# State-space heads: group sums of squares on VectorE, output products one slot later, decay sums split between GpSimd and ScalarE

## The reference, cut to what matters

```python
gate, hbc, dt = jnp.split(x @ in_proj_w.T, [I, I + CD], axis=-1)      # I = 32 * 128
hs, B, C = jnp.split(silu(causal_conv4(hbc) + conv_b), [I, I + G * N], axis=-1)
dt = softplus(dt + dt_bias);  A_cum = cumsum(-exp(A_log) * dt)        # along the sequence
# head h uses group h % 8 of B and C; over l >= s:
y[l] = sum_s (C[l] . B[s]) * exp(A_cum[l] - A_cum[s]) * dt[s] * X[s] + D * X[l]
h32 = y * silu(gate)
var = mean(h32 ** 2 over the 512 channels of a norm group (4 heads))
out = (norm_w * h32 * rsqrt(var + EPS)) @ out_proj_w.T
```

## Time and profile before

| what | us |
|---|---|
| median of 3 runs | 3315.8 (3304.01 to 3317.79) |
| the profiled execution's own time | 3299.21 |
| its span in the trace | 3297.4 |
| first half's heads, first `px` to last `px` | 148.8 to 640.8 |
| second half's heads, first `px` to last `px` | 766.6 to 1258.6 |
| TensorE busy over the span | 2619.4 (79%) |
| VectorE, ScalarE, GpSimd busy | 1809.8, 1525.4, 1227.2 |

### The profile page before, as it was taken

How to read it: one execution, slowest core, us unless ns; L and a number is a source line. 1 busy time by engine, 2 the same in 40 slices (tenths; PEclk the granted TensorE clock), 3 DMA queues, 4 the chain that set the end, 5 groups by cost and what they waited for, 6 DMA issues and landing times. The chain is left out here.

```text
span 3297.4 us, 47157 instructions
## 1 busy us (share of the span) xinstructions
PE 2619.4 (79%) x13661; PEld 1670.5 (51%) x13663; DVE 1809.8 (55%) x3839; ACT 1525.4 (46%) x2975; POOL 1227.2 (37%) x1164
## 2 busy tenths in 40 slices
PE   4799999987999996577777937878557749698884
PEld 2467777744777775344444523333244414365552
DVE  4666666674666664788882146776223342133234
ACT  3555555564555552588891114655235410233321
POOL 0477777635777773000000020000000027344443
PEclk8999999998999997666657957999679868799997
DMA  1121211002221210740000000000000024587885
GB/s 61 52 52 33 59 48 36 14 14 58 58 52 33 58 26 26 250 136 1 1 1 31 0 18 1 1 1 1 23 0 0 0 81 158 129 177 172 175 172 126
DMA packets 127073, 192.74 MB, mean 58 GB/s; under 512 B 17552, under 2 KB 88208, under 8 KB 125584
## 3 DMA queue, kind: packets, MB, share of 16 engines
q1 hardware_dynamic: 83696, 134.71, 14.5%
q0 software_dynamic: 23616, 33.24, 5.8%
q10 hardware_dynamic: 19584, 22.57, 2.5%
HBM read 123.23 MB, written 67.25 MB: 58 GB/s over the span
## 5 line engine op out<-in xcount | busy, mean ns | idle before, releaser
L234 DVE SCALAR_TENSOR_TENSOR h_pre<-h_px,h_par,h_pre 128x510 f32<-128x510 f32 (+2 forms) x384 | 286.5, 746 | 269.1 <-ACT h_pre L695 249.2
L658 PE MATMUL h_po<-h_wo,h_h 128*128 128x256 f32 x1024 | 328.2, 411 | 0.0
L580 POOL TENSOR_SCALAR h_decay<-h_cumb,h_sel 128x256 f32<-128x256 f32 x256 | 290.9, 1136 | 25.2 <-DMA h_cumb<-cum_rows 25.2
L591 POOL TENSOR_TENSOR h_mix<-h_decay,cb 128x768 f32<-128x768 f32 x128 | 232.8, 1819 | 165.0 <-ACT h_decay L681 165.0
L2890 POOL DMA_INDIRECT moe_sums<-ex_y,ex_sidx x132 | 204.8, 1552 | 234.7 <-DVE ex_y L3069 216.6
L622 PE MATMUL h_px<-x_cols,h_w 128*128 128x512 f32 x512 | 254.4, 620 | 25.3 <-DMA h_d<-d_skip 25.3
L849 POOL TENSOR_TENSOR norm_rstd<-norm_mv,mhalf 128x4 f32<-128x4 f32 x24 | 28.3, 1178 | 605.3 <-DVE norm_mv L832 605.3
L627 PE MATMUL h_pz<-x_cols,h_w 128*128 128x512 f32 x512 | 242.5, 596 | 5.6 <-DVE h_gate L748 5.6
L707 ACT ACTIVATE h_xt<-h_pxt,h_sel 128x128 f32<-128x128 f32 x512 | 145.9, 368 | 151.9 <-PE h_pxt L646 151.9
L2942 PE MATMUL ex_pg<-ex_w,ex_xT 128*128 x528 | 194.7, 492 | 25.6 <-ACT ex_xT L2998 10.5
L660 PEld LDWEIGHTS h_pss<-ones,h_sq 128*128 128x128 f32 x1024 | 194.6, 190 | 26.3
(11 more groups left out here) (389 smaller groups left out, 5809.6 us busy)
## 6 DMA issues: line engine op xcount, KB each, us to landing
h_cumb<-cum_rows SPq DMA_DIRECT2D x32, 1024.0 KB, 8.6
moe_tiles<-blank SPq DMA_DIRECT2D x4, 6642.0 KB, 44.2
ex_w<-moe_w SPq DMA_DIRECT2D x64, 352.0 KB
ex_xg<-moe_tiles ACTq DMA_DIRECT2D x136, 162.0 KB, 2.6
ex_wd<-moe_wd SPq DMA_DIRECT2D x64, 176.0 KB
h_w<-w_xg SPq DMA_DIRECT2D x8, 1024.0 KB, 10.5
moe_sums<-blank SPq DMA_DIRECT2D x2, 2176.0 KB, 26.6
h_wo<-w_out SPq DMA_DIRECT2D x8, 512.0 KB, 10.3
```

What stands on the lines that cost most here:

```text
L234: ins = dve.scalar_tensor_tensor(out=out[:, :, back:S], in0=src[:, :, 0:S - back], scalar=par[:, at + CK - 1 - back:at + CK - back], in1=o ...
L580: pool.tensor_scalar(decay[j][:, u, 0:S], cumb[s.vb][:, j, u, :], sel[s.vb][:, u * TPB, 1, j:j + 1], 0.0, ALU.subtract, ALU.min)
L591: pool.tensor_tensor(mix[j % 2][:], decay[j][:], cbj, ALU.mult).then_inc(matched, 1)
L658: pe.matmul(po[t // TPB][:, t % TPB, :], hh[j % 2][:, t * P:(t + 1) * P], w_out[s.pg][:, j, :], start=(j == 0 and t % TPB == 0), stop=(j = ...
```

## The change

- The loops and `LEAD` go: each engine's list is written out for all 16 steps, with constant counts and addresses. (The loops before ran once or twice around bodies that were written out as well.)
- `out` of head k moves from slot k to slot k+1, at the slot's end as before: `parts` of TensorE reads (-1, out). `hh` gets four buffers in place of two.
- The squares of j = 0 are written to a tile `sqs`, those of j = 1 to 3 to `sq`, and VectorE adds these three to `sqs` (`total`, one 128x512 instruction each, in the slot after the head's). TensorE multiplies `sqs` by the ones once per step, after the output product of j = 3.
- `variance` and `add` move from slot j = 0 to slot j = 1 of the next step on VectorE, `variance` ahead of the convolution, `add` behind the gate; `root` moves on GpSimd from slot j = 0, ahead of match and argue, to slot j = 1, behind them.
- GpSimd's `argue` writes only the two diagonal 128x128 blocks of each sequence (four instructions of 128x128); ScalarE's `decays` writes the block below the diagonal as Exp of `cumb` with the bias `less` (minus the column's sum, which `select` prepares), two instructions of 128x128, and then Exp of the diagonal blocks, one of 512 columns.
- `group` runs ahead of the first `argue`, and later in the middle of the group before; SyncE's `cumb` load waits for `decayed` in place of `argued`.

```diff
@@ Step, head_turns -> STEPS, head_slots (counts and addresses become constants) @@
+        less = [sb(f"less{i}", [P, TW, HG]) for i in range(2)]
-        hh = [sb(f"h{i}", [P, 2 * S]) for i in range(2)]
+        hh = [sb(f"h{i}", [P, 2 * S]) for i in range(HG)]
         sq = [sb(f"sq{i}", [P, 2 * S]) for i in range(2)]
+        sqs = [sb(f"sqs{i}", [P, 2 * S]) for i in range(2)]
...
@@ gpsimd @@
                 for u in range(2):
-                    pool.tensor_scalar(decay[j][:, u, 0:S], cumb[s.vb][:, j, u, :], sel[s.vb][:, u * TPB, 1, j:j + 1], 0.0,
-                                       ALU.subtract, ALU.min)
-                    ins = pool.tensor_scalar(decay[j][:, u, S:TRI], cumb[s.vb][:, j, u, P:S], sel[s.vb][:, u * TPB + 1, 1, j:j + 1], 0.0,
-                                             ALU.subtract, ALU.min)
+                    for b in range(TPB):
+                        ins = pool.tensor_scalar(decay[j][:, u, 2 * b * P:(2 * b + 1) * P], cumb[s.vb][:, j, u, b * P:(b + 1) * P],
+                                                 sel[s.vb][:, u * TPB + b, 1, j:j + 1], 0.0, ALU.subtract, ALU.min)
...
-                    if j == 0:
-                        root(prev)
-                    slot(parts, cur, nxt, j)
+            def body(k):
+                if k % (HG * NP) == HG * NP // 2 and k // HG + NP // 2 < len(STEPS):
+                    group(STEPS[k // HG + NP // 2])
+                slot(((2, match), (3, argue)), k)
+                if k % HG == 1 and k > HG:
+                    root(STEPS[k // HG - 1])
+
+            group(STEPS[0])
+            head_slots(-3, 0, body)
...
@@ tensor, out @@
-                pe.wait_ge(squared, LEAD + h + 1)
                 if j == 0:
-                    pe.wait_ge(added, LEAD + s.n)
+                    after(pe, added, s.n)
                 for t in range(TW):
-                    pe.matmul(po[t // TPB][:, t % TPB, :], hh[j % 2][:, t * P:(t + 1) * P], w_out[s.pg][:, j, :],
-                              start=(j == 0 and t % TPB == 0), stop=(j == HG - 1), skip_group_check=True)
-                    mm = pe.matmul(pss[:, t:t + 1], sq[j % 2][:, t * P:(t + 1) * P], r.ones[:, 0:1],
-                                   start=(j == 0 and t == 0), stop=(j == HG - 1), skip_group_check=True)
+                    mm = pe.matmul(po[t // TPB][:, t % TPB, :], hh[j][:, t * P:(t + 1) * P], w_out[s.pg][:, j, :],
+                                   start=(j == 0 and t % TPB == 0), stop=(j == HG - 1), skip_group_check=True)
                 mm.then_inc(outed, 1)
-            parts = ((3, project), (1, scan), (2, turn), (0, out))
+                if j == HG - 1:
+                    pe.wait_ge(totalled, (s.n + 1) * (HG - 1))
+                    after(pe, vared, s.n)
+                    for t in range(TW):
+                        mm = pe.matmul(pss[:, t:t + 1], sqs[s.vb][:, t * P:(t + 1) * P], r.ones[:, 0:1], start=True, stop=True)
+                    mm.then_inc(pooled, 1)
+            parts = ((3, project), (1, scan), (2, turn), (-1, out))
@@ scalar @@
-                act.activation(decay[j][:], decay[j][:], ACT.Exp).then_inc(decayed, 1)
+                for u in range(2):
+                    act.activation(decay[j][:, u, P:S], cumb[s.vb][:, j, u, P:S], ACT.Exp, bias=less[s.vb][:, u * TPB, j:j + 1])
+                own = decay[j][:].rearrange("p u (b l) -> p u b l", l=P)[:, :, 0:3:2, :]
+                act.activation(own, own, ACT.Exp).then_inc(decayed, 1)
...
@@ vector @@
+            def total(s, j, h):
+                if j:
+                    dve.wait_ge(squared, h + 1)
+                    dve.tensor_tensor(sqs[s.vb][:], sqs[s.vb][:], sq[j % 2][:], ALU.add).then_inc(totalled, 1)
...
-                    finish(*head(cur, nxt, j))
-                    if j == 0:
-                        variance(prev)
-                    slot(((2, silu),), cur, nxt, j)
-                    if j == 0:
-                        if nxt:
-                            select(nxt)
-                        add(prev)
-                    slot(((3, conv), (3, open_)), cur, nxt, j)
+                slot(((0, finish), (-1, total), (2, silu)), k)
+                if j == 0 and n + 1 < len(STEPS):
+                    select(STEPS[n + 1])
+                if j == 1 and n >= 1:
+                    variance(STEPS[n - 1])
+                slot(((3, conv), (3, open_)), k)
+                if j == 1 and n >= 1:
+                    add(STEPS[n - 1])
```

More of the change, by code:

```diff
@@ L414, with __init__, head_slots, at_head @@
 class Step:
[L417 to L442, removed]
+    def __init__(self, n):
+        self.n = n
+        self.g, self.p = divmod(n, NP)
+        self.g2, self.pg = divmod(self.g, 2)
+        self.two, self.vb = divmod(self.p, 2)
+STEPS = [Step(n) for n in range(GH * NP)]
+def head_slots(first, last, body):
+    for k in range(first, len(STEPS) * HG + last):
+        body(k)
+def at_head(h):
+    return (STEPS[h // HG], h % HG, h) if 0 <= h < len(STEPS) * HG else None
 def mamba_heads(nc, a, r, half, cum_rows, dtc, cb):
@@ L522, in mamba_heads, with slot, group @@
         block = ctx2.enter_context(nc.Block())
[L524 to L529, removed]
+        def slot(parts, k):
             for ahead, part in parts:
-                at = head(cur, nxt, j + ahead)
-                if at:
-                    part(*at)
+                if at_head(k + ahead):
+                    part(*at_head(k + ahead))
         @block.sync
         def _(sp):
-            def group(g2, pg):
-                sp.wait_ge(added, LEAD + (g2 * 2 + pg - 1) * NP)
-                g = (g2 * 2 + pg) * 2 + half
+            def group(s):
+                pg = s.pg
+                after(sp, added, (s.g - 1) * NP)
+                g = s.g * 2 + half
                 sp.dma_start(w_in[pg][:], a["w_xg"][g]).then_inc(loaded[pg], 16)
@@ L547, in cum, with group @@
             def cum(s):
-                sp.wait_ge(argued, LEAD + (s.n - 1) * HG)
+                after(sp, decayed, (s.n - 1) * HG)
                 sp.dma_start(cumb[s.vb][:].rearrange("p j u l -> p j (u l)"),
                              cum_rows[bass.ds((s.g * 2 + half) * HG, HG), bass.ds(s.p * 2 * S, 2 * S)].partition_broadcast(P)).then_inc(cums[s.vb], 16)
[L553 to L559, removed]
+            for s in STEPS:
+                if s.p == 0:
+                    group(s)
+                cum(s)
+            sp.wait_ge(added, len(STEPS))
         @block.gpsimd
         def _(pool):
-            for one in (scaled, matched, argued):
-                pool.drain().then_inc(one, LEAD)
             pool.memset(halves[:], 0.5)
             pool.drain()
-            pool.drain().then_inc(rooted, LEAD - 1)
-            def group(g2, pg):
-                pool.wait_ge(loaded[pg], (g2 + 1) * 64)
+            def group(s):
+                pg = s.pg
+                pool.wait_ge(loaded[pg], (s.g2 + 1) * 64)
                 pool.tensor_tensor(dskip[pg][:], dskip[pg][:], halves[:], ALU.mult)
@@ L593, in root @@
             def root(s):
[L594 to L595 removed]
+                pool.wait_ge(vared, s.n + 1)
+                after(pool, added, s.n)
                 pool.tensor_tensor(rstd[:], var[:], r.mhalf[:, 0:TW], ALU.pow).then_inc(rooted, 1)
[L598 to L604 removed]
@@ L606, in _ @@
-            for j in range(-3, 0):
-                slot(parts, Step(0, 0, 0, 0), None, j)
-            head_turns(pool, body, group)
-            root(Step(GH // 2 - 1, 1, NP // 2 - 1, 1))
+            def body(k):
[5 more added lines that the diff above has]
+            group(STEPS[0])
@@ L611, in _ @@
+            head_slots(-3, 0, body)
+            root(STEPS[-1])
         @block.tensor
         def _(pe):
-            for one in (projected, gprojected, turned, scanned, outed):
-                pe.drain().then_inc(one, LEAD)
             def project(s, j, h):
-                if s.opens and j == 0:
+                if s.p == 0 and j == 0:
                     pe.wait_ge(loaded[s.pg], (s.g2 + 1) * 64)
-                pe.wait_ge(convolved, LEAD + h - 1)
+                after(pe, convolved, h - 1)
```

130 lines of the change are left out of this document (58 added, 72 removed).

## The result

Slower, by less than forecast. The kernel after took 3332.1 us (median of 7 runs, 3317.0 to 3341.3), the kernel before 3314.0 beside it (7 runs, 3304.0 to 3317.8). The ratio is 1.0056 [1.0038, 1.0075]: +18 us where +45 were forecast. The profiled executions are 3328.4 and 3299.2, with spans of 3326.6 and 3297.4, +29.2. The heads carry nearly all of that: from the first `px` of a half to its last add, 514.0 and 514.1 us have become 528.7 and 525.9, together +26.6.

What follows compares the result with a forecast made beforehand. The heads were taken as bound by TensorE's own work. Waits +11.1, two steps without -5.4, starts -10.4 and clock +49.5 sum to +44.8 us, on the median 3315.8 giving 3361; range 3302 to 3395 (8 in 10).

Steps and rivals of the forecast that it cites:

- the chain: From the turn in slot j = 0 through ScalarE, GpSimd and VectorE to TensorE's output product: 10.87 us, 7.80 covered, 3.07 waited.
- TensorE's own work: In the heads, a step of four heads falls by 2.70 to 28.50 us, before any wait.
- which nothing gives back: Behind each of 30 new TensorE waits, a 3.3 us stretch at half clock loses 1.65 us: +49.5 us.
- The starts: At each half's start, TensorE's 3.56 us wait and the slow stretch behind it go: 5.2 each, -10.4 us.
- These I set to nothing, 0 to 5 us either way: Small effects, among them VectorE's `total`, ScalarE's extra time, GpSimd's `group` in mid-group and SyncE's loads: set to nothing.
- Rival one: In the heads, the same 3.07 us wait but the clock holds: 3311 us, no change; chance 0.15.
- Rival two: VectorE's queue alone sets the wait, about 2.3 us, clock kept: step 30.8, whole 3288 us; chance 0.13.
- Rival three: Two slow stretches behind each wait in the heads, +49.5 us more: 3410 us; chance 0.17.

Runs made afterwards that it cites:

- e5_onein: e1_early with GpSimd's match reading one tile: it copies the decay and leaves out the product with `cb`; 3203.6 us, 0.9654 of the kernel before.
- e3_fill: The kernel after with six products of 256 columns, results unread, put on TensorE ahead of the wait for the add; 3306.6 us, 0.9996 of the kernel before.
- e1_early: e2_root with the add moved right behind the variance, ahead of the convolution, on VectorE; 3253.6 us, 0.9828 of the kernel before.
- e2_root: The kernel after with root alone moved ahead of match and argue on GpSimd; 3280.4 us, 0.9925 of the kernel before.
- e6_square_first: e1_early with ScalarE's square put ahead of the exponentials in a slot, all work kept; 3236.0 us, 0.9745 of the kernel before.

## Why the prediction was half right

The sign and the chain were right, the size was not: +18 by the medians and +29 in the two profiled executions, where +45 were forecast. The step that failed is the clock's price behind every wait: forecast 30 x 1.65 = 49.5, measured 16 x 1.69 = 27.0.

- **TensorE's own work**, 28.50 us a step: right, 28.59 in the steps with a wait. The covered part of the chain was forecast as 7.80 and is 7.80; e5_onein shows the whole step without waits.
- **The chain**, 10.87 us: 10.52. Three exponentials 1.22 for 1.15 (nearer to the 1.19 that the prediction worked out from the Trainium skill, ScalarE: Activation LUTs, and put beside its own figure), argue 2.74 for 2.76, add 1.66 for 1.66. The one term that was off is root: 1.02, not the 1.40 of the earlier trace rows. That row was itself stretched: before, root ran into VectorE's `h_xs`, as the timeline of the kernel before shows:

```profile
453.81 0.68 DVE L754 SCALAR_TENSOR_TENSOR h_xs<-h_tx,h_pre 128x512 f32<-128x512 f32 x1
```

  Root began at 453.98 and ended 0.89 behind the end of `h_xs`. In the kernel after it stands beside the gate (439.54), which reads one SBUF tile and one of PSUM, and is not held.
- **"which nothing gives back", 30 x 1.65 = +49.5**: this step failed. The price of a fall was right (1.69), and so was its meaning: e3_fill is even, and in place of the idle time it has work and no fall. What failed is that every wait would cost it. I took a wait of about 2.9 as shown, saw 2.71 with a fall and 2.25 without in the earlier trace rows, and read a sure loss from them. More rows of that stage would not have warned: all seven of its waits of 2.61 to 2.95 lost the clock and none of the seven of 2.25 to 2.41 did. But they come in one beat, about every 24 us, so they are not seven independent trials, and another beat can give another share. The ordinary waits came out at 2.55, between those rows, and lost the clock 8 times in 20; with the longer ones it is 16 in 30. The text named "waits that lose the clock not every time" only within the range.
- **The starts**, -10.4: right, -10.5.
- **"These I set to nothing, 0 to 5 us either way"**: wrong for `group` and `total`, which meet on GpSimd and VectorE. The waits of steps with `group` are about 1.2 longer, and each of them loses the clock, in both traces; and the meetings hold e1_early above its bound.
- **Rival one**, 3311 if the clock holds: e3_fill, 0.9996, is that case. **Rival two**, 3288: e2_root, with the step of 30.8 that was worked out for it; root is early there, as that rival needs. **Rival three** (two slow stretches): not seen; a fall cost one.

Open: why one wait of 2.55 loses the clock and the next, as long, does not. The steps differ between two traces of the same kernel, so it isn't a property of the step. That the 2.25 us wait of the earlier trace rows kept the clock was no proof either: 4 of 28 waits of 2.0 to 2.2 lost it. Open too is why a fall is missing behind a wait of 3.2 and not behind one of 2.0.

## What to carry to other kernels

Work taken from the bounding engine is worth nothing while a chain through the other engines sets the pace: follow the chain to where it meets that engine again, and move its last links (here root and add) first. A wait that recurs between dense stretches of TensorE is priced twice, once as the wait and once as the clock behind it, and the second price can be a share of the times (16 of 30 here) or every time (seven of seven in a later stage of the kernel before). Before giving VectorE an instruction that reads two SBUF tiles, look which GpSimd instruction will run beside it; reordering the one against the other (e6_square_first) was worth 0.8% here.

## What was not expected of the hardware

- A VectorE instruction that reads two SBUF tiles and a GpSimd instruction that reads one or two don't share the time: whichever starts later ends about its own duration behind the other. `h_h`, `total` and `h_xs` (128x512 f32, 0.69 alone) take up to 2.35 beside a GpSimd instruction of 1.8 to 1.9, less where they start late in it; the other way round a match takes 2.38 (370.17), root 1.40 and the four parts of argue 3.75 (364.52) in place of 2.77. VectorE's `less`, 128x16, which reads one SBUF tile, took 1.78 beside a match in e1_early (195.05) in place of 0.17, so two tiles are not needed. The Trainium skill (GPSIMD Engine Reference, section 1. Specifications) says that GpSimd shares its SBUF interfaces with VectorE and that they contend when VectorE reads two SBUF inputs or works in a mode that uses two ports; that section gives no size. The traces agree for two inputs, and put the size at the whole rest of the other instruction; in which mode `less` worked, no trace shows.
- The convolution on VectorE, which reads PSUM and SBUF, kept its mean of 746 ns in both kernels, beside match and argue too.
- GpSimd goes over 128x768 f32 with two constant operands in 0.88 us on average (e5_onein), where 128x256 with a scalar per partition takes 1.14.
